# Four-layer graph network on one core: one-hots and tile loads of the pass by source regrouped, batch norm's scale moved into a weight, transposes copied by the vector engine

## The reference, cut to what matters

```
# layer 0: a filter per edge; messages go from dst (col) to src (row)
messages = h[dst] * fsum                       # fsum: one number per edge
agg      = segment_sum(messages, src)
out      = softplus(agg @ Wi1 + bi1) @ Wi2 + bi2
out      = gamma * (out - mov_mean) * rsqrt(mov_var + 1e-3) + beta
x        = x + out
# layers 1 and 3: graph attention (layer 1 has two steps, one head; layer 3 has 8 heads)
hw = h @ W ;  logit = leaky_relu(a_src[src] + a_dst[dst])
e  = exp(logit - bound[dst])                   # the kernel takes a bound over all nodes
x_att = segment_sum(hw[src] * e, dst) / segment_sum(e, dst)
# layer 2: messages = MLP([h[src], edge_attr, global]), mean over dst, an update MLP, a layer norm
```

## Time and profile before

| | |
|---|---|
| median of 3 runs | 7402.07 us |
| the profiled execution | 7404.54 us |
| its span in the profile | 7402.5 us |
| PE, DVE, ACT, POOL busy | 45%, 45%, 23%, 68% of the span |
| granted TensorE clock, mean | 0.645 of full speed |

### The profile page before, as it was taken

The page is one execution under the profiler, slowest core; times in us unless marked ns, Lnnn a source line. Parts: engine busy times, 40 slices in busy tenths (PEclk is TensorE's granted clock), DMA queues, the critical chain, the costliest instruction groups (busy, mean ns, idle before and its releaser), DMA issues. The chain is left out here.

```text
span 7402.5 us, 89274 instructions
## 1 busy us (share of the span) xinstructions
PE 3331.8 (45%) x17325; PEld 2957.3 (40%) x17326; DVE 3299.0 (45%) x10231; ACT 1691.6 (23%) x4176; POOL 5000.4 (68%) x5176
## 2 busy tenths in 40 slices
PE   2200000444443864444434444445777775444443
PEld 1100000444443753444434444434777664344443
DVE  8777732333323663333344333335333336544445
ACT  2200000211111963222223222223222224000000
POOL 1677777677777726777755777764777770777775
PEclk9655555666666986555556555566666677666666
DMA  6122234444443624444434444433444440444443
GB/s 225 57 92 91 96 97 151 153 156 156 155 154 133 218 79 136 129 134 131 133 91 129 133 133 130 133 100 107 134 135 134 134 128 30 132 132 133 132 132 105
DMA packets 507505, 942.53 MB, mean 127 GB/s; under 512 B 204347, under 2 KB 240683, under 8 KB 507304
## 3 DMA queue, kind: packets, MB, share of 16 engines
q1 hardware_dynamic: 349288, 637.41, 25.9%
q0 software_dynamic: 158144, 304.31, 15.8%
HBM read 673.90 MB, written 270.84 MB: 128 GB/s over the span
## 5 line engine op out<-in xcount | busy, mean ns | idle before, releaser
L1371 POOL DMA_INDIRECT edge_buf<-node_table,ixr x1664 | 1571.6, 944 | 619.4 <-issue 507.9
L1371 POOL DMA_INDIRECT Y<-node_table,ixr x1664 | 1569.7, 943 | 521.1 <-issue 519.9
L1111 DVE TENSOR_TENSOR ACC<-ACC,bank 128x129 f32 (+2 forms) x3744 | 1092.9, 292 | 1102.2 <-PE bank L1098 469.2
L1279 POOL DMA_INDIRECT layer_messages<-edge_buf,ixr x832 | 809.3, 973 | 295.7 <-issue 263.0
L1538 PE MATMUL bank<-adc,turned_buf 128*128 x2496 | 340.3, 195 | 1476.1 <-issue 571.7
L440 POOL DMA_INDIRECT edge_records<-edge_buf x782 | 791.2, 1012 | 255.1 <-issue 246.2
L1538 PEld LDWEIGHTS bank<-adc,turned_buf 128*128 128x128 bf16 x2496 | 257.0, 103 | 1606.7 <-issue 1552.4
L1098 PE MATMUL bank<-edge_buf,Y 128*128 128x129 f32 (+2 forms) x3744 | 821.1, 406 | 142.7 <-ACT edge_buf L1524 96.5
L1098 PE MATMUL bank<-Y 128*128 128x129 f32 (+1 forms) x3328 | 763.1, 420 | 158.6 <-ACT Y L1524 88.7
L1098 PEld LDWEIGHTS bank<-edge_buf,Y 128*128 128x128 f32 x3744 | 764.0, 309 | 173.1 <-DVE ACC L1111 136.7
L1098 PEld LDWEIGHTS bank<-Y 128*128 128x128 f32 x3328 | 713.4, 323 | 181.5 <-issue 89.0
(11 more groups left out here) (279 smaller groups left out, 5319.1 us busy)
## 6 DMA issues: line engine op xcount, KB each, us to landing
Y<-onehots SPq DMA_DIRECT2D x416, 512.0 KB, 3.6
turned_buf<-onehots_turned SPq DMA_DIRECT2D x312, 256.0 KB, 3.8
edge_buf<-edge_records SPq DMA_DIRECT2D x208, 288.0 KB, 2.9
onehots<-Y SPq DMA_DIRECT2D x104, 512.0 KB, 2.7
layer_messages<-ACC SPq DMA_DIRECT2D x28, 1584.0 KB
XI<-layer_messages SPq DMA_DIRECT2D x78, 528.0 KB, 3.7
edge_records<-H SPq DMA_DIRECT2D x1, 29952.0 KB
onehots_turned<-turned_buf SPq DMA_DIRECT2D x104, 256.0 KB
```

Of the source, the lines that this page charges most:

```text
L1111: nc.vector.tensor_tensor(acc, acc, places.at(q, j, w), ALU.add).then_inc(added, 1)
L1279: pool.indirect_dma_start(msg_d, bass.IndirectOffsetOnAxis(ap=ixr[h][:, j:j + 1], axis=0), rows[h][:, j, 0:MW], None, bounds_check=SLOTS - ...
L1371: pool.indirect_dma_start(ring[q][:, j, 0:w], None, table, bass.IndirectOffsetOnAxis(ap=ixr[q][:, j:j + 1], axis=0)).then_inc(rows_in[q], 16)
```

## The change

It has five parts.

1. `layer0_src_pass`, DVE: the offsets of two halves are loaded by one instruction, 16 at once, ahead of the first of the two; the function that adds is split so that it takes offsets already loaded.
2. `layer0_src_pass`, one-hots: POOL and ACT make those of 7 of the 8 halves of a round. DVE makes the eighth in one operation (is_equal against the column numbers, which it has put into PSUM bank 0 once), between its fourth and its fifth half of adds.
3. POOL, at the end of `layer0_src_pass`: a memset of gmax and one `partition_all_reduce` over it, whose result nobody uses.
4. Setup multiplies Wi2 by bn_scale, column by column; `after0` loses its product with bn_scale and adds PSUM to X directly.
5. In the three node products with `normed` and no `before`, DVE copies the transposes to SBUF in place of ACT: the copy of group g + 1 stands ahead of the taking of group g.

```
@@ setup, DVE @@
   st.then(v.tensor_tensor(bn_shift[:, :], bn_shift[:, :], bn_scale[:, :], ALU.mult))
+  st.then(v.tensor_tensor(mat["Wi2"][0][:, :], mat["Wi2"][0][:, :], bn_scale[:, :], ALU.mult))
@@ node_product @@
+  dve_copies = normed is not None and before is None
+  def copy(g):
+      dve.wait_ge(turned, g + 1)
+      if g >= turns:
+          dve.wait_ge(prod, 2 * (g - turns) + 2)
+      v.tensor_copy(stT[g % 2][:, :], bank[g % 2][:, :]).then_inc(turned_sb, 1)
   prepare(0)
   prepare(1)
+  if dve_copies:
+      copy(0)
   for g in range(NG):
       if g + 2 < NG:
           prepare(g + 2)
+      if dve_copies and g + 1 < NG:
+          copy(g + 1)
       take_product(dve, v, then, g, prod, taken, cols, after)
...
-                        if g + 1 < NG:
+                        if g + 1 < NG and not dve_copies:
                             copy(g + 1)
@@ node_tiles @@
-                tiles[0:1, bass.ds(n * G, G)], engines=[engine], min_val=0,
+                tiles[0:1, bass.ds(n * G, halves * G)], engines=[engine], min_val=0,
@@ layer0_src_pass, POOL and ACT @@
-                        for q in range(deep):
+                        for q in range(by_vector):        # deep = 8, by_vector = 7
...
+                    nc.gpsimd.memset(gmax[:, :], 0.0).then_inc(gmax_set, 1)
+                    pool.wait_ge(gmax_set, 1)
+                    pool.partition_all_reduce(gmax_all[:, :], gmax[:, :], P, bass.bass_isa.ReduceOp.max).then_inc(gmax_set, 1)
+                    pool.wait_ge(gmax_set, 2)
@@ layer0_src_pass, DVE @@
+                    nc.vector.tensor_copy(bank[0][:, 0:P], iota_row[:, :]).then_inc(iota_in_psum, 1)
-                    looped(dve, rounds, lambda i, first: [
-                        add_sums(dve, i * deep + q, q, two_sets, sums, acc_of_s, D, summed, i * deep + q + 1, added)
-                        for q in range(deep)])
+                    def onehot_here(i, q):
+                        dve.wait_ge(msg_in[q], i * 16 + 16)
+                        dve.wait_ge(summed, i * deep + q - oh_deep + 1)
+                        nc.vector.tensor_tensor(tiles_of_half(onehots[q]), bank[0][:, 0:P].unsqueeze(1).to_broadcast([P, G, P]),
+                                                by_tile[q][:, :, D:D + 1].to_broadcast([P, G, P]), ALU.is_equal) \
+                            .then_inc(oh_ready[q], 1)
+                    def body(i, first):
+                        for pair in range(deep // 2):
+                            n = i * deep + 2 * pair
+                            at = node_tiles(mybir.EngineType.DVE, acc_of_s, n, 2)
+                            for k in range(2):
+                                add_to(dve, n + k, 2 * pair + k, two_sets, sums, at[k * G:k * G + G], D, summed, n + k + 1, added)
+                            if 2 * pair + 1 == by_vector - oh_deep:
+                                onehot_here(i, by_vector)
+                    looped(dve, rounds, body)
@@ after0 @@
-                then(v.tensor_tensor(ACC[:, at, 0:D], rows_psum, columns(bn_scale, 2), ALU.mult))
-                then(v.tensor_tensor(X[:, at, :], X[:, at, :], ACC[:, at, 0:D], ALU.add))
+                then(v.tensor_tensor(X[:, at, :], X[:, at, :], rows_psum, ALU.add))
```

More of the change, by code:

```diff
@@ L933, in _ @@
                             normed(g).then_inc(norm_done, 1)
-                    copy(0)
+                    if not dve_copies:
+                        copy(0)
                     for g in range(NG):
@@ L1067, in gnn, with node_tiles @@
         sums = [ACC[:, :, :].rearrange("p b w -> p (b w)"), Hflat]
-        def node_tiles(engine, tiles, n):
+        def node_tiles(engine, tiles, n, halves=1):
             return nc.values_load_multi_w_load_instructions(
-                tiles[0:1, bass.ds(n * G, G)], engines=[engine], min_val=0,
+                tiles[0:1, bass.ds(n * G, halves * G)], engines=[engine], min_val=0,
                 max_val=(NODE_TILES - 1) * (AW if tiles is not tile_of_d else 1),
@@ L1102, in add_sums, with add_to @@
         def add_sums(dve, n, q, places, accs, tiles, w, summed, signals, added):
-            at = node_tiles(mybir.EngineType.DVE, tiles, n)
+            add_to(dve, n, q, places, accs, node_tiles(mybir.EngineType.DVE, tiles, n), w, summed, signals, added)
+        def add_to(dve, n, q, places, accs, at, w, summed, signals, added):
             dve.wait_ge(summed, signals)
@@ L1283, in _ @@
                         pool.wait_ge(sent[h], 16 * G * ITERS)
+        gmax, gmax_all = sb("gmax", [P, 8]), sb("gmax_all", [P, 8])
         def layer0_src_pass():
@@ L1290, in layer0_src_pass @@
                                                  ("msg_in", "apart", "distance", "oh_ready"))
-            summed, added, odd_cleared = sem("summed"), sem("added"), sem("odd_cleared")
+            gmax_set = sem("gmax_set")
+            summed, added, odd_cleared, iota_in_psum = (sem(n) for n in ("summed", "added", "odd_cleared", "iota_in_psum"))
             msg_v = msg_d.rearrange("(k p j) w -> k p (j w)", p=P, j=G)
@@ L1298, in layer0_src_pass @@
             rounds = HALVES // deep
+            by_vector = deep - 1
             with nc.Block() as block:
@@ L1331, in body @@
                     def body(i, first):
-                        for q in range(deep):
+                        for q in range(by_vector):
                             act.wait_ge(apart[q], i + 1)
@@ L1343, in _ @@
                     nc.vector.memset(H[:, :, :], 0.0).then_inc(odd_cleared, 1)
+                    nc.vector.tensor_copy(bank[0][:, 0:P], iota_row[:, :]).then_inc(iota_in_psum, 1)
                     dve.wait_ge(odd_cleared, 1)
-                    looped(dve, rounds, lambda i, first: [
-                        add_sums(dve, i * deep + q, q, two_sets, sums, acc_of_s, D, summed, i * deep + q + 1, added)
-                        for q in range(deep)])
+                    dve.wait_ge(iota_in_psum, 1)
+                    def onehot_here(i, q):
[13 more added lines that the diff above has]
+                    looped(dve, rounds, body)
                 @block.tensor
@@ L1374, in gnn @@
         a_dst, den = sb("a_dst", [P, NBP * 8]), sb("den", [P, NBP * 8])
-        gmax, gmax_all = sb("gmax", [P, 8]), sb("gmax_all", [P, 8])
         def by_head(t, heads):
```

## The result

The changed kernel takes 7368.3 us (median of 5 runs, 7366.65 to 7380.72), the one before 7401.49 on the same chip (5 runs, 7399.5 to 7413.68): ratio 0.9957, 95% interval 0.9944 to 0.9969, 33.2 us faster. The forecast was 7352, 50 us faster. The time is in the forecast's range of 7342 to 7375, but not in the 7342 to 7364 that stood for the forecast's own mechanism, and a third of the gain did not come. Where it is missing is read stage by stage.

A forecast was written before the change was run, and what follows sets the result against it. DVE with its queue was taken to bound the pass by source, POOL's gathers the edge passes. Terms -29.8 - 8.0 - 12.0 - 0.5 = -50.3 us from 7402.07 gave 7351.8, say 7352; range 7342 to 7375.

The forecast's parts named there:

- the forecast's own mechanism: Whole kernel: all five parts gain as reckoned, -50.3 us to 7352, own range 7342 to 7364; chance 0.80.
- The mechanism in the pass by source: Pass by source: DVE with its queue stays the bound, rounds fall from 20.4 to 18.0 us, -29.8 us in all.
- a load by the word: Rival, pass by source: three of four loads a round cost 0.60 us more, round 19.9 us, time 7375; chance 0.10.
- The forecast's other sign: Pass by source: the forecast is wrong if an engine other than DVE ends the waits in a round.
- I take 0.60, since so even a time looks like a fixed one: DVE's load of 16 offsets, pass by source: 0.60 us like the load of 8; bounds 0.60 and 1.20.
- The Trainium skill's floor of about 600 ns: DVE's offset loads: the skill's page gives tensor_load a floor of about 600 ns, matching the 598 ns row for 8 words.
- forecast 1.53: DVE's transition with the one-hot, pass by source: 0.3 for two waits + 1.225 us, load hidden, in place of 1.02.
- The 1 us counted for the first round: Unrolled first round of the pass by source: fills with the clock low and waits for PE, counted as 1 us of gain.
- The "6.6 us later" of the bound: End of the pass by source: if nothing hid POOL's early maximum, the stage would end 6.6 us later.
- the terms 1.02 + 0.69 + 0.2: Layer 1's node product, one DVE group: taking 1.02, copy 0.69, waits some 0.2; 1.9 us in place of 2.01.
- twelve full steps: Layer 1's node product: first take at 2768.09 + 12 x 1.87 = 2790.5, against 2790.67 before.
- The other two: Rivals: POOL's early maximum not hidden or paid again, 7360, chance 0.07; 16 offsets not fitting registers, 7427, chance 0.03.

The follow-up runs named there:

- the packed kernel: Changed kernel with all one-hots on POOL and ACT, adds waiting on constants, and two 16-bit offsets packed per word; 8966.53 us against 8972.4 before, on the slower chip.

## Why the prediction was off, step by step

The mechanism in the pass by source failed, though the time fell into the range. The forecast itself named rounds above 19 us as the sign that it was wrong, and they are 19.7. 7368 is 7 us from the 7375 of the rival "a load by the word" and 16 from the forecast's 7352; it is in the range because that was drawn out to 7375, in part for this rival's sake, and not through the mechanism. The forecast's other sign, waits ended by an engine other than DVE, shows in the releasers too (49.5 us by PE); PE's timeline and the load at 2575.41, read above, explain it.

- **Part 1, one load for two halves.** The steps around the load were right: a transition without one is 0.30 us as estimated, and 52 loads of 16 are there. The step that failed is its second paragraph, "I take 0.60, since so even a time looks like a fixed one": the load measures 1.10 us. The evenness of 104 rows that all load 8 words tells nothing on 16. With the fourth load behind the one-hot, the part brings 4 x 0.72 - 3 x 0.50 = 1.4 us a round, not 2.9; with all four open, as in the experiment without the one-hot, 0.9. The Trainium skill's floor of about 600 ns (DMA: Bandwidth & Descriptors, Latency and other measured facts) matched the row by chance of its 8 words: 4 words take 0.35 us here, so it is no floor.
- **Part 2, a one-hot on DVE.** It takes 1.22 us, and the load runs beside it, as said. The transition is 1.71, forecast 1.53: a load of 16 and the queue's work around it end a little behind the one-hot. With parts 1 and 2 the account closes: three open loads at +0.50 and one at +0.18 are 1.68 us a round, and 18.0 + 1.68 = 19.7, the round measured. Times 12 that is 20 of the 20.4 us by which the pass missed. The 1 us counted for the first round isn't shown: from its first add to the next round's it takes 19.62 us before, and 18.82 and 19.82 in the two traces of the changed instructions. DVE stayed the bound, as forecast; the experiment without the one-hot shows that the part was worth nothing as long as DVE is (0.17 us a round lost).
- **Part 3, POOL's maximum.** Right in mechanism and gain: -7.9 against -8.0, hidden, and not paid again by the later passes. But in its new place the operation waits 5.9 us behind the memset, where the forecast reckoned with 8.6; so 6.4 us of cover were needed and not 9.1. Why the first use waits longer at the start of the attention pass no run shows. The "6.6 us later" of the bound takes the margin from the cost; with nothing hidden it would be the whole 9.1 us.
- **Part 4, the scale.** Right: -12.05 against -12.0.
- **Part 5, the copies.** Right mechanism, mis-sized: 2 to 3 us gained, forecast 0.5. The wait between take and copy is 0.21 us as assumed. But in layer 1 groups come 1.83 us apart (2768.12 to 2769.95), where the terms 1.02 + 0.69 + 0.2 make 1.91 and the forecast went on with 1.87; and it took twelve full steps, though the last group is only 1.15 us behind its forerunner after the change as well (2769.95 to 2771.10). From the first take to the last, in the mean of the eight traces with the part and the two without, layer 1's product takes 22.5 and 23.1 us, layer 2's 21.1 and 23.0, layer 3's 23.3 and 23.2. That is -0.6, -1.8 and +0.1, where -0.2, -0.9 and +0.5 were forecast.
- **The rivals.** "A load by the word" is what happened; it forecast rounds of 19.9 (with 1.20 for the load) and 7375, against 19.7 and 7368. It had a chance of 0.10. One row at one size gave no ground for putting it that low. The other two did not happen: the maximum stayed hidden, and the adds kept their 0.21 us, so the 16 offsets fitted.

## What to carry to other kernels

A duration that is always the same in a trace is a fixed cost only if the size varied; where all rows have one size, both ends of the bound deserve a large chance. Merging loads into registers saves what is paid once (here 0.10 us and the operations around it, 0.22 us for each load saved), not the words, and one long pause costs more than two short ones when the engine ahead has only two buffers to fill. A signal that frees a buffer belongs to the last instruction that uses it, not to one behind the next load.

## What the runs showed of the hardware

- POOL's first `partition_all_reduce` of the program begins 5.9 us behind the instruction ahead of it inside the pass by source, and 7.9 to 8.6 us behind DVE's maximum where it stands at the start of the attention pass. Once it has been used, it begins 0.4 us behind DVE's maximum in layer 1. The cost is paid once.
- TENSOR_LOAD from SBUF into DVE's registers: 0.35, 0.60, 1.10 and 2.10 us for 4, 8, 16 and 32 words, but 0.31 to 0.56 for one word and 0.53 for two. It runs beside an instruction that its engine is executing (a load of 1.10 us begun 0.1 us into a one-hot of 1.22: together 1.71 us from add to add, 1.52 for the load alone).
- DVE's adds to alternating accumulators, each waiting for the one two back, start 0.21 us apart at a duration of 0.29, with or without a 40 ns register operation ahead of each; the unpacking of the packed kernel makes it 0.25 in the mean.
- The chips differ. On the slowest the kernel before takes 8972 us, against 7401 and 7404 on those of the other two sets; the pass by source has the same rounds (19.71 us), but the first attention pass takes 1228 us from first to last gather, against 1037 to 1040. POOL's groups by line there, in that pass:
```profile
L1421 POOL DMA_INDIRECT Y<-node_table,ixr x415 | 391.4, 943 | 226.5 <-issue 131.3 <-remote 95.2
```
On the chip of the first experiments a gather's instruction takes the same 943 ns and no idle time of POOL in that pass has the releaser "remote". What it is isn't settled here. It shows that a time can only be held against one of the same chip.
